# Turning the mask bytes of a graph attention kernel on TensorE as four-byte float32r words instead of two-byte bfloat16 words

## The chip, the cores and the metric

The kernel runs on one NeuronCore of a Trainium2 chip. The metric is the device time of one execution in microseconds (us), lower is better. TensorE is called PE here, its weight loads PEld, VectorE is DVE, ScalarE is ACT, GpSimd is POOL and SyncE is SP.

## The reference

Two graph layers over 8192 nodes with 128 features. The first is an attention with a 0/1 adjacency mask, the second a plain product with the same adjacency.

```python
    h = jnp.maximum(_layernorm(x, axis=-1), 0.0)
    x = x + _L0_gnn_ref(h, adj, L0_gnn_cmt_weight, L0_gnn_W, L0_gnn_a1, L0_gnn_a2)
    h = jnp.maximum(_layernorm(x, axis=-1), 0.0)
    x = x + _L1_gnn_ref(h, adj, L1_gnn_W1, L1_gnn_W2, L1_gnn_b)
```

```python
        Wh = inputs @ W
        f1 = Wh @ a1
        f2 = Wh @ a2
        e = jax.nn.leaky_relu(f1 + f2.T, negative_slope=ALPHA)
        scores = jnp.where(adj > 0, e, NEG_INF)
        att = jax.nn.softmax(scores, axis=-1)
        node_out = jax.nn.relu(att @ Wh)
```

```python
        node = h @ W1
        hw = jnp.einsum('nc,kcf->nkf', h, W2)
        x = jnp.einsum('nk,nkf->nf', node, hw)
        x = adj @ x
        x = x + node @ b
```

## The kernel before

The adjacency is 8192 x 8192 float32 (268 MB), read once. Its 8 x 8 blocks of 1024 x 1024 are walked in 64 half turns: 8 blocks of rows (`ib`), and for each 8 blocks of columns, two (`p` = 0, 1) to a turn `jg`. One half turn works so:

- SP loads the block in two halves of 2 MB into `adj_sb` (four buffers `q`).
- ACT casts it to bytes of 0 or 64 in `m8` (L508, four instructions of 2048 elements a row in a half turn). `m8[:, p, t, n]` has on each of 128 partitions 8 rows `t` of 1024 column bytes.
- PE turns the bytes (`turn_mask`, L751 to L760). It takes two neighbouring bytes as one bfloat16 word and transposes 128 x 128 words at a time; the mode moves the words without arithmetic. A bank of PSUM (`mt_ps0`, `mt_ps1` in turns) takes eight such transposes, and four banks (`k` = 0 to 3, C = 4) make up the half turn. Bank `k` holds the words k, k + 4, k + 8 and so on of all eight rows.
- ACT copies each bank to `mt[:, p, k, :]` (`evict`, L520). When all four are there, they are also stored to `maskT_d` for the second layer (L626, 1 MB).
- DVE forms the attention weights (`weigh`, L1008): per bank two instructions, one per byte of the words (`b_`), each 1024 elements, max(z, q) times the mask byte. It writes one of four buffers of `p_sb`.
- PE multiplies them with the rows of `wh` (L824): per buffer 8 float32 products of 129 columns, each two instructions, added up in `ot_ps`.

A **step** below is one `k` of a half turn: PE turns a bank that is of the step after next, and then does the products of two `p_sb` buffers (32 MATMULs). In the half turns of the last seven blocks of rows, PE, ACT, DVE and POOL also finish one tile of 128 nodes of the block before: layer norm, the sixteen heads of the second layer (L789 on PE, L585 on ACT, sums on POOL), in pieces at k = 0 to 3.

The program of each engine is in a fixed order written out by hand; engines meet by semaphores. `turned` counts banks turned, `evicted` banks copied, `p_ready` buffers weighed, `p_used[r]` buffers multiplied, `adj_cast[q]` casts done, `mt_stored[p]` stores landed.

In the second part (adjacency stage, `gather`, L881) the stored bytes are loaded again, ACT (L612) and DVE (L1048) widen them to float32r words `mask32`, and PE multiplies them, 512 columns at a time, with the messages in `msgs` (float32r too).

Of the kernel before, what the change touches and what calls it, by code (L numbers as in the profile page):

```python
# [38 lines left out]
def build(nc, x, adj, W, a1, a2, W1, W2, b, out):  # L39
# [25 lines left out]
    with ctx:  # L65
# [6 lines left out]
        def sem(name):  # L72
# [6 lines left out]
        msgs_at = nc.sbuf_base - 4 * (NT * (D + 2) + BLK * T // 2 + C * BLK)  # L79
        msgs = nc.alloc_sbuf_tensor_at("msgs", [P, NT, 2, D], FP32R, offset=msgs_at)  # L80
# [10 lines left out]
        ident16 = sb("ident16", [P, P], BF16)  # L91
# [37 lines left out]
            .rearrange("p (s c n b) -> p s c n b", s=2, c=C, b=2)  # L129
# [15 lines left out]
            .rearrange("p (s i c n b) -> p s i c n b", s=4, i=2, c=C, b=2)  # L145
# [217 lines left out]
        def _(pool):  # L363
# [3 lines left out]
            pool.memset(ident16[:, :], 0.0).then_inc(consts, 1)  # L367
            pool.wait_ge(consts, 2)
            for m in (ident, ident16):
                pool.affine_select(out=m[:, :], in_=m[:, :], compare_op=ALU.not_equal, fill=1.0, base=0,  # L370
                                   pattern=[[-1, P]], channel_multiplier=1).then_inc(consts, 1)
# [98 lines left out]
        def _(act):  # L470
# [74 lines left out]
            act.activation(bcol[:, :], fcol[:, :, 1], ACT.Exp, bias=shifts[:, 0:1]).then_inc(setup_act, 1)  # L545
            for h in range(2):
                act.wait_ge(z0_done, h + 1)
                act.activation(zbf[:, h * HB:(h + 1) * HB], hw_ps[h][:, :], ACT.Copy).then_inc(z0_copied, 1)

            evict(1, 1, 0, 0)  # L550
# [6 lines left out]
            act.dma_start(zrow_d, zT[:, :]).then_inc(z_stored, 16)  # L557

# [46 lines left out]
            def convert(ii, first, t):  # L605
                s, r = t // T, t % 2
                for ib in range(2):
                    if not on_dve(first, t, ib):
                        act.wait_ge(masks_in[s % 4], 16 * (ii * (NB // 4) + s // 4 + 1))
                        if not (first and t < 2):  # L610
                            act.wait_ge(conv_used[r][ib], ii * (NT // 2) + t // 2)
                        act.activation(mask32[:, r, ib, :], masks[:, s % 4, ib, t % T // 2, :, t % 2], ACT.Copy)\  # L612
                           .then_inc(conv_act, 1)

            def turn(i, ib, jg, finish, last):
                for p in range(2):
                    n = 2 * i + p
                    for k in range(C):

                        if k < 2:  # L620
                            evict(C * n + k + 2, k + 2, p, 0)
                        elif not (last and p == 1):
                            evict(C * n + k + 2, k - 2, 1 - p, i + p)
# [75 lines left out]
        def _(pe):  # L699
# [49 lines left out]
            def turn_mask(chunk, k, p, casts):  # L749

                if k == 0:  # L751
                    for h in range(2):
                        pe.wait_ge(adj_cast[2 * p + h], casts)
                if not (isinstance(chunk, int) and chunk < 2):
                    pe.wait_ge(evicted, chunk - 1)
                words = mt_ps[k % 2][:, :].bitcast(BF16)
                for t in range(T):
                    ins = pe.transpose(words[:, t * P:(t + 1) * P],  # L758
                                       m8[:, p, t, :].bitcast(BF16)[:, k:BLK // 2:C], ident16[:, :])
                ins.then_inc(turned, 1)  # L760
# [16 lines left out]
            pe.transpose(h_ps[0:NT, D:D + P], zcol[:, :], ident[:, :]).then_inc(setup_pe, 1)  # L777

# [21 lines left out]
            def half_turn(ib, jg, p, finish, last):  # L800
# [6 lines left out]
                for k in range(C):  # L807
                    if k < 2:
                        turn_mask(C * n + k + 2, k + 2, p, 0)
                    elif not (last and p == 1):  # L810
                        turn_mask(C * n + k + 2, k - 2, 1 - p, i + 1 + p)
# [93 lines left out]
        def _(dve):  # L905
# [98 lines left out]
            def weigh(n, i, ib, p, k, b_, tile):  # L1004

                r = 2 * (k % 2) + b_
                dve.wait_ge(p_used[r], 4 * i + 2 * p + k // 2)
                dve.scalar_tensor_tensor(p_sb[:, r, :], zbf[:, bass.ds((ib % 2) * BLK, BLK)],  # L1008
                                         qcol[:, bass.ds(tile + b_, 1)], mtb[:, p, k, :, b_],
                                         ALU.max, ALU.mult).then_inc(p_ready, 1)  # L1010

            def turn(i, ib, jg, finish, last):
                for p in range(2):
                    n = 2 * i + p
                    u = i - IT
                    for k in range(C):
                        c = C * n + k
                        tile = (2 * jg + p) * T + 2 * k
                        dve.wait_ge(evicted, c + 1)
# [11 lines left out]
            def start_weights(ib):  # L1031

                if isinstance(ib, int) and ib == 0:
                    dve.wait_ge(z0_copied, 2)
                else:
                    dve.wait_ge(zb_in, 16 * ib)
                dve.wait_ge(evicted, C * NB * ib + 1)
                for b_ in range(2):
                    weigh(NB * ib, IT * ib, ib, 0, 0, b_, 0)

            def convert(ii, first, t):
                s, r = t // T, t % 2
                for ib in range(2):
                    if on_dve(first, t, ib):
                        dve.wait_ge(masks_in[s % 4], 16 * (ii * (NB // 4) + s // 4 + 1))
                        if not (first and t < 2):
                            dve.wait_ge(conv_used[r][ib], ii * (NT // 2) + t // 2)
                        dve.tensor_copy(mask32[:, r, ib, :], masks[:, s % 4, ib, t % T // 2, :, t % 2])\  # L1048
                           .then_inc(conv_dve, 1)
# [88 lines left out]
```

## Time and profile before

| | us |
|---|---|
| median of 3 runs | 1843.87 (1843.55 to 1845.21) |
| the profiled execution's own time | 1848.05 |
| its span in the trace | 1846.4 |
| PE busy (weight loads PEld) | 1814.0 (1578.9) |
| ACT, DVE, POOL busy | 1328.9, 1202.2, 695.8 |
| start of the attention's products | 60.5 |
| end of the last turned bank | 1310 |

The span is measured from the first to the last instruction of the profiled execution. MATMULs are pipelined, so a MATMUL's recorded duration is longer than its turn on the array: the pace is read from start to start. An instruction of an engine is recorded with its source line; a row names what it writes and reads, the count behind x, and the idle time of the engine just before with what ended it.

### The profile page before, as it was taken

Reading aid. Unit: us, or ns where it says so; the run is one execution under the profiler, and the core shown is the slowest. Engines: PE = TensorE matmul, PEld = TensorE weight load, DVE = VectorE, ACT = ScalarE, POOL = GpSimd, SP = SyncE. Lnnn points to the kernel's source line nnn. Section 1 sums busy time; section 2 is a strip of 40 time slices with the busy share of each in tenths; the row PEclk is TensorE's granted clock in tenths of the full one; section 3 lists DMA queues with packets and bytes.
Section 4 is the critical chain, followed back from the end, with each engine's and each line's share of the span. In section 5 each row is a group of like instructions: output and inputs, shape, how many; then the busy total and the mean of one; then the engine's idle time right before and its main releaser. Section 6 shows DMA issues by size and latency. Waiting matters only on the chain.

```text
span 1846.4 us, 38424 instructions
## 1 busy us (share of the span) xinstructions
PE 1814.0 (98%) x13344; PEld 1578.9 (86%) x13344; DVE 1202.2 (65%) x1519; ACT 1328.9 (72%) x2145; POOL 695.8 (38%) x524
## 2 busy tenths in 40 slices
PE   8999999999999999999999999999999999999998
PEld 5899989889988988998898889889867788888886
DVE  7676677767767776776777677767665543443434
ACT  6766788788788778877887887887456655555554
POOL 0000256556545655664565556446544400000000
PEclk9999999999999999999999999999999999999999
DMA  9788867776776777677767767772933344345330
GB/s 331 293 347 315 325 244 287 288 283 253 292 294 257 272 293 292 241 291 294 271 259 298 288 251 278 291 279 109 384 122 146 146 160 183 139 177 206 148 148 23
DMA packets 105809, 452.19 MB, mean 245 GB/s; under 512 B 6736, under 2 KB 15136, under 8 KB 87968
## 3 DMA queue, kind: packets, MB, share of 16 engines
q1 hardware_dynamic: 86720, 356.53, 51.9%
q10 hardware_dynamic: 12208, 75.62, 10.0%
q0 software_dynamic: 6832, 19.41, 2.9%
q8 instruction: 29, 0.48, 0.1%
q14 instruction: 20, 0.16, 0.0%
HBM read 364.46 MB, written 87.07 MB: 245 GB/s over the span
## 4 chain that ended last, share of the span: by engine, by line
PE 89%; DVE 3%; ACT 2%; issue 2%; SPq 1%; DMA 1%; POOL 1%; DVEq 0%; POOLq 0%; ACTq 0%
PE ot_ps L824 46%; PE mt_ps L881 12%; PE ot_ps L881 12%; PE hw_ps L789 11%; PE mt_ps L758 6%; SPq L292 1%; PE h_ps L784 1%; DVE att L984 1%; DVE p_sb L1008 1%; ACT prod L585 1%; DMA adj_sb<-in_adj_dram 1%; POOL prod L390 1%; DMA keep_d<-keep 1%; ACT wh_mask L508 1%; DVE keep L989 0%
## 5 line engine op out<-in xcount | busy, mean ns | idle before, releaser
L824 PE MATMUL ot_ps<-wh_mask,p_sb 128*128 (+1 forms) x8192 | 978.5, 277 | 9.2 <-DVE p_sb L1008 9.2
L824 PEld LDWEIGHTS ot_ps<-wh_mask,p_sb 128*128 128x128 f32 x8192 | 939.9, 192 | 11.4 <-DVE p_sb L1008 10.9
L1008 DVE SCALAR_TENSOR_TENSOR p_sb<-zb,qcol,mt 128x1024 f32<-128x1024 uint8 (+1 forms) x512 | 771.0, 1536 | 266.0 <-ACT mt L520 218.0
L390 POOL TENSOR_TENSOR prod<-prod 128x1024 f32<-128x1024 f32 (+2 forms) x192 | 404.4, 2106 | 521.0 <-ACT prod L585 503.8
L508 ACT ACTIVATE wh_mask<-adj_sb 128x2048 uint8<-128x2048 f32 x256 | 493.0, 1929 | 1.7 <-ACT mt L520 1.1
L612 ACT ACTIVATE mask<-adj_sb 128x1024 fp32r<-128x1024 uint8 x240 | 255.5, 1065 | 176.5 <-PE ot_ps L881 176.4
L520 ACT ACTIVATE mt<-mt_ps 128x1024 uint16<-128x1024 uint16 x256 | 267.7, 1046 | 136.5 <-PE mt_ps L758 135.8
L1048 DVE CAST mask<-adj_sb 128x1024 fp32r<-128x1024 uint8 x272 | 204.1, 756 | 247.4 <-PE mt_ps L881 245.6
L585 ACT ACTIVATE prod<-hw_ps,node 128x128 f32<-128x128 f32 x1024 | 278.9, 385 | 92.5 <-PE hw_ps L789 91.5
L881 PE MATMUL mt_ps<-mask,msgs 128*128 128x512 f32 x1024 | 283.3, 398 | 3.6 <-DVE mask L1048 2.7
L881 PE MATMUL ot_ps<-mask,msgs 128*128 128x512 f32 x1024 | 275.5, 391 | 0.7
L789 PE MATMUL hw_ps<-wcat,hT 128*128 128x512 f32 x512 | 240.7, 592 | 0.0
L881 PEld LDWEIGHTS mt_ps<-mask,msgs 128*128 128x128 f32 x1024 | 191.7, 188 | 52.7 <-issue 14.3
L881 PEld LDWEIGHTS ot_ps<-mask,msgs 128*128 128x128 f32 x1024 | 192.3, 188 | 43.3 <-issue 3.0
L758 PEld LDWEIGHTS mt_ps<-ident,wh_mask 128*128 128x128 bf16 x2048 | 143.5, 114 | 61.8 <-issue 61.8
L758 PE MATMUL mt_ps<-ident,wh_mask 128*128 128x128 bf16 x2048 | 156.0, 219 | 0.6 <-issue 0.6
L789 PEld LDWEIGHTS hw_ps<-wcat,hT 128*128 128x128 f32 x512 | 88.6, 190 | 61.8 <-issue 61.2
L393 POOL TENSOR_TENSOR msg<-prod 128x128 f32<-128x128 f32 x64 | 82.2, 1284 | 5.0
L418 POOL DMA_DIRECT2D zb<-zrow_d x7 | 3.8, 544 | 179.3 <-DVE p_sb L1008 119.6
L407 POOL TENSOR_TENSOR msg<-msg 128x128 fp32r<-128x128 f32 x56 | 68.0, 1215 | 4.5
L405 POOL CAST msg<-msg 128x128 fp32r<-128x128 f32 x56 | 58.9, 1051 | 9.3 <-POOL msg L393 9.3
L575 ACT ACTIVATE node<-h_ps 128x16 f32<-128x16 f32 x64 | 11.8, 185 | 54.9 <-PE h_ps L784 54.9
(111 smaller groups left out, 610.8 us busy)
## 6 DMA issues: line engine op xcount, KB each, us to landing
adj_sb<-in_adj_dram SPq DMA_DIRECT2D x128, 2048.0 KB, 8.6
maskT_d<-mt ACTq DMA_DIRECT2D x64, 1024.0 KB, 5.2
adj_sb<-maskT_d SPq DMA_DIRECT2D x32, 2048.0 KB, 7.7
keep_d<-keep POOLq DMA_DIRECT2D x64, 128.0 KB, 6.1
p_sb<-keep_d SPq DMA_DIRECT2D x4, 2048.0 KB, 12.2
msg_d<-msg POOLq DMA_DIRECT2D x56, 128.0 KB, 6.0
msgs<-msg_d SPq DMA_DIRECT2D x7, 1024.0 KB, 9.1
wh_mask<-in_x_dram SPq DMA_DIRECT2D x8, 512.0 KB, 9.4
```

The costliest lines, as they stand in the source:

```text
L390: pool.tensor_tensor(prod[:, 0:n, :], prod[:, 0:n, :], prod[:, n:2 * n, :], ALU.add)\
L393: pool.tensor_tensor(msg32[:, :], prod[:, 0, :], prod[:, 1, :], ALU.add).then_inc(prod_read, 1)
L508: ins = act.activation(m8[:, q // 2, t:t + HT // 2, :].rearrange("p t n -> p (t n)"), adj_sb[:, q, part * (HT // 2) * BLK:(part + 1) * (HT ...
L520: act.activation(mt[:, p, k, :], mt_ps[k % 2][:, :].bitcast(U16), ACT.Copy).then_inc(evicted, 1)
L585: ins = act.activation(prod[:, head, :], hw_ps[g % 2][:, j * D:(j + 1) * D], ACT.Copy, scale=node[:, head:head + 1])
L612: act.activation(mask32[:, r, ib, :], masks[:, s % 4, ib, t % T // 2, :, t % 2], ACT.Copy)\
L758: ins = pe.transpose(words[:, t * P:(t + 1) * P], m8[:, p, t, :].bitcast(BF16)[:, k:BLK // 2:C], ident16[:, :])
L789: pe.matmul(hw_ps[g % 2][:, :], hT[:, :], wcat[:, g * HB:(g + 1) * HB], start=True, stop=True)\
L824: ins = pe.matmul(ot_ps[h][:, (t - t0) * ROW:(t - t0 + 1) * ROW], p_sb[:, r, t * P:(t + 1) * P], rows, start=begin and t == t0, stop=end a ...
L881: ins = pe.matmul(acc_ps[2 * ib + h][:, :], msgs[:, ORDER[s] * T + t % T, c, :], mask32[:, r, ib, h * HB:(h + 1) * HB], start=t == 0 and c ...
L1008: dve.scalar_tensor_tensor(p_sb[:, r, :], zbf[:, bass.ds((ib % 2) * BLK, BLK)], qcol[:, bass.ds(tile + b_, 1)], mtb[:, p, k, :, b_], ALU.m ...
L1048: dve.tensor_copy(mask32[:, r, ib, :], masks[:, s % 4, ib, t % T // 2, :, t % 2])\
```

## The change

`turn_mask` reads `m8` through a second name for the same bytes, `m8_words`, typed float32r: four neighbouring bytes are one word. A bank then takes four transposes of 128 x 128 words of four bytes instead of eight of two bytes; it is as full as before (2 KB a partition). Bank `k` now holds every second word (k // 2) of four of the eight rows (k % 2). The identity is a float32r tile, `identr`. Since a weigh needs all eight rows of its byte column, DVE needs two banks, k and k + 1, before an even k; so each bank is turned and evicted one step sooner: at step k the bank of k + 3, not k + 2. A third bank is turned ahead of the loop. The first half of the cast rows (`adj_cast[2 * p]`) is now enough for bank 0, and the second half is waited for at bank 1. DVE and ACT read the bytes of `mt` and of `maskT_d` with a stride of 4 bytes instead of 2.

```diff
+        m8_at = nc.sbuf_base - 4 * (BLK * T // 2 + C * BLK)
+        m8_words = nc.alloc_sbuf_tensor_at("m8_words", [P, 2, T, BLK // 4], FP32R, offset=m8_at)
...
-        ident16 = sb("ident16", [P, P], BF16)
+        identr = sb("identr", [P, P], FP32R)
...
-            .rearrange("p (s c n b) -> p s c n b", s=2, c=C, b=2)
+            .rearrange("p (s c n b) -> p s c n b", s=2, c=2, b=4)
...
+            evict(1, 1, 0, 0)
             for h in range(2):
                 act.wait_ge(z0_done, h + 1)
                 act.activation(zbf[:, h * HB:(h + 1) * HB], hw_ps[h][:, :], ACT.Copy).then_inc(z0_copied, 1)
 
-            evict(1, 1, 0, 0)
...
+            evict(2, 2, 0, 0)
...
-                        act.activation(mask32[:, r, ib, :], masks[:, s % 4, ib, t % T // 2, :, t % 2], ACT.Copy)\
+                        act.activation(mask32[:, r, ib, :], masks[:, s % 4, ib, t % T // 4, :, t % 4], ACT.Copy)\
...
-                        if k < 2:
-                            evict(C * n + k + 2, k + 2, p, 0)
+                        if k == 0:
+                            evict(C * n + 3, 3, p, 0)
                         elif not (last and p == 1):
-                            evict(C * n + k + 2, k - 2, 1 - p, i + p)
+                            evict(C * n + k + 3, k - 1, 1 - p, i + p)
...
-                if k == 0:
-                    for h in range(2):
-                        pe.wait_ge(adj_cast[2 * p + h], casts)
+                if k < 2:
+                    pe.wait_ge(adj_cast[2 * p + k], casts)
                 if not (isinstance(chunk, int) and chunk < 2):
                     pe.wait_ge(evicted, chunk - 1)
-                words = mt_ps[k % 2][:, :].bitcast(BF16)
-                for t in range(T):
+                words = mt_ps[k % 2][:, :].bitcast(FP32R)
+                for t in range(HT):
                     ins = pe.transpose(words[:, t * P:(t + 1) * P],
-                                       m8[:, p, t, :].bitcast(BF16)[:, k:BLK // 2:C], ident16[:, :])
+                                       m8_words[:, p, k % 2 * HT + t, k // 2:BLK // 4:2], identr[:, :])
                 ins.then_inc(turned, 1)
...
+            turn_mask(2, 2, 0, 1)
...
-                    if k < 2:
-                        turn_mask(C * n + k + 2, k + 2, p, 0)
+                    if k == 0:
+                        turn_mask(C * n + 3, 3, p, 0)
                     elif not (last and p == 1):
-                        turn_mask(C * n + k + 2, k - 2, 1 - p, i + 1 + p)
+                        turn_mask(C * n + k + 3, k - 1, 1 - p, i + 1 + p)
...
-                                         qcol[:, bass.ds(tile + b_, 1)], mtb[:, p, k, :, b_],
+                                         qcol[:, bass.ds(tile + b_, 1)], mtb[:, p, k // 2, :, 2 * (k % 2) + b_],
...
-                        dve.wait_ge(evicted, c + 1)
+                        dve.wait_ge(evicted, C * n + 2 * (k // 2) + 2)
```

The order of PE at the start of the attention, before (L758 is the transposes, L824 the products, `h_ps` a small bank of the set-up):

```order
L776 MATMUL h_ps<-wx_sb,small 128x128
L777 MATMUL h_ps<-ident,zcol 64x128
L758 MATMUL mt_ps<-ident,wh_mask 128x128 x8
L824 MATMUL ot_ps<-wh_mask,p_sb 128x129 x16
L758 MATMUL mt_ps<-ident,wh_mask 128x128 x8
```

The same place of the changed program, where L760 is the transposes and L827 the products:

```order
L778 MATMUL h_ps<-wx_sb,small 128x128
L779 MATMUL h_ps<-ident,zcol 64x128
L760 MATMUL mt_ps<-identr,m_words 128x128 x8
L827 MATMUL ot_ps<-wh_mask,p_sb 128x129 x16
L760 MATMUL mt_ps<-identr,m_words 128x128 x4
```

Before, the loop's first bank has eight transposes and the set-up none; now two banks of four stand together here (the extra bank turned ahead, and the loop's first), and every later step has four. An entry of these lists stands for one instruction of the program; a float32 product is two MATMULs in the trace.

The order of ACT in the first rolled turn at k = 1 and k = 2, before, with what each row waits for (L520 evicts a bank, L508 casts, L626 stores, `ISA` and `REGISTER_ALU` set registers):

```order
L520 ACTIVATE mt<-mt_ps 128x1024 [waits turned]
L505 ISA
L508 ACTIVATE wh_mask<-adj_sb 128x2048 [waits turned,adj_in0]
L516 REGISTER_ALU
L518 REGISTER_ALU [waits turned]
L519 REGISTER_ALU [waits p_ready]
L520 ACTIVATE mt<-mt_ps 128x1024 [waits mt_stored1]
L626 ISA [waits evicted]
L626 DMA maskT_d<-mt 128x4096
```

The same place now (L522, L510 and L629 in their stead):

```order
L520 REGISTER_ALU [waits turned]
L521 REGISTER_ALU [waits p_ready]
L522 ACTIVATE mt<-mt_ps 128x1024 [waits mt_stored1]
L507 ISA
L510 ACTIVATE wh_mask<-adj_sb 128x2048 [waits turned,adj_in0]
L518 REGISTER_ALU
L522 ACTIVATE mt<-mt_ps 128x1024 [waits turned]
L629 ISA [waits evicted]
L629 DMA maskT_d<-mt 128x4096
```

The eviction that opens a new `mt` buffer, and so waits for that buffer's store, moved from k = 2 to k = 1; the place of the store itself did not move, and each step still has one eviction.

## Rows read from the trace of the kernel before

**Rows 1.** The page, part 1: busy us, share of the span, instructions.
```profile
PE 1814.0 (98%) x13344; PEld 1578.9 (86%) x13344; DVE 1202.2 (65%) x1519; ACT 1328.9 (72%) x2145; POOL 695.8 (38%) x524
```

**Rows 2.** The page, part 4: shares of the chain that ended last.
```profile
PE 89%; DVE 3%; ACT 2%; issue 2%; SPq 1%; DMA 1%; POOL 1%; DVEq 0%; POOLq 0%; ACTq 0%
PE ot_ps L824 46%; PE mt_ps L881 12%; PE ot_ps L881 12%; PE hw_ps L789 11%; PE mt_ps L758 6%; SPq L292 1%; PE h_ps L784 1%; DVE att L984 1%; DVE p_sb L1008 1%; ACT prod L585 1%; DMA adj_sb<-in_adj_dram 1%; POOL prod L390 1%; DMA keep_d<-keep 1%; ACT wh_mask L508 1%; DVE keep L989 0%
```

**Rows 3.** Busy us by stage, one half turn third: PE, PEld, DVE, ACT, POOL.
```profile
60.00:190.00 130.00, 128.91 (x1261) 128.75 (x1262) 90.65 (x73) 94.73 (x71) 1.10 (x2) 1.00 0.87 333
190.00:1300.00 1110.00, 1102.41 (x9378) 988.65 (x9377) 807.80 (x847) 885.76 (x1544) 609.70 (x435) 1.00 0.72 272
1043.20:1063.30 20.10, 20.10 (x172) 18.02 (x171) 14.70 (x16) 16.14 (x29) 11.71 (x8) 1.00 0.72 274
1300.00:1846.00 546.00, 533.24 (x2399) 427.89 (x2396) 262.64 (x383) 310.72 (x448) 82.48 (x74) 0.99 0.42 162
```

**Rows 4.** The page, part 5, PE: busy us, mean ns | idle before.
```profile
L824 PE MATMUL ot_ps<-wh_mask,p_sb 128*128 (+1 forms) x8192 | 978.5, 277 | 9.2 <-DVE p_sb L1008 9.2
...
L758 PE MATMUL mt_ps<-ident,wh_mask 128*128 128x128 bf16 x2048 | 156.0, 219 | 0.6 <-issue 0.6
```

**Rows 5.** Timeline of PE, one half turn: start us, us, what.
```profile
1043.23 0.61 PE L758 MATMUL mt_ps<-ident,wh_mask 128*128 128x128 bf16 x8
1043.67 3.79 PE L824 MATMUL ot_ps<-wh_mask,p_sb 128*128 x32
1047.30 0.61 PE L758 MATMUL mt_ps<-ident,wh_mask 128*128 128x128 bf16 x8
...
1055.56 0.41 PE L784 MATMUL h_ps<-wcat,hT 128*128 128x144 f32 x2
...
1061.60 1.88 PE L789 MATMUL hw_ps<-wcat,hT 128*128 128x512 f32 x4
1063.32 0.61 PE L758 MATMUL mt_ps<-ident,wh_mask 128*128 128x128 bf16 x8
```

**Rows 6.** Timeline of PE, transposes of the results at 1485 us.
```profile
1485.22 1.03 PE L853 MATMUL hw_ps<-ident,prod 128*128 128x128 f32 x8
1486.09 0.60 PE L853 MATMUL ot_ps<-ident,prod 128*128 128x128 f32 x4
```

**Rows 7.** Timeline of PE, adjacency stage: 512-column products.
```profile
1432.44 1.08 PE L881 MATMUL mt_ps<-mask,msgs 128*128 128x512 f32 x4
1433.36 1.07 PE L881 MATMUL ot_ps<-mask,msgs 128*128 128x512 f32 x4
```

**Rows 8.** Weight loads by form: busy us, mean ns | idle before.
```profile
L824 PEld LDWEIGHTS ot_ps<-wh_mask,p_sb 128*128 128x128 f32 x8192 | 939.9, 192 | 11.4 <-DVE p_sb L1008 10.9 <-issue 0.5
L881 PEld LDWEIGHTS ot_ps<-mask,msgs 128*128 128x128 f32 x1024 | 192.3, 188 | 43.3 <-issue 3.0
...
L853 PEld LDWEIGHTS hw_ps<-ident,prod 128*128 128x128 f32 x32 | 3.7, 140 | 1.6 <-ACT prod L657 1.2
...
L766 PEld LDWEIGHTS h_ps<-ident,ext 128*2 128x2 f32 x1 | 0.1, 81 | 0.5 <-DVE ext L942 0.5
```

**Rows 9.** Timeline of ACT, the same half turn.
```profile
1052.18 1.02 ACT L520 ACTIVATE mt<-mt_ps 128x1024 uint16<-128x1024 uint16 x1 [1.22 <-PE mt_ps L758]
...
1054.90 0.27 ACT L561 ACTIVATE hT<-h_ps 128x128 f32<-128x128 f32 x1
...
1060.68 1.07 ACT L520 ACTIVATE mt<-mt_ps 128x1024 uint16<-128x1024 uint16 x1
```

**Rows 10.** Timeline of DVE, the same half turn.
```profile
1045.89 3.07 DVE L1008 SCALAR_TENSOR_TENSOR p_sb<-zb,qcol,mt 128x1024 f32<-128x1024 uint8 x1 [0.25 <-PE ot_ps L824]
...
1061.90 1.28 DVE L1008 SCALAR_TENSOR_TENSOR p_sb<-zb,qcol,mt 128x1024 f32<-128x1024 uint8 x1 [4.57 <-ACT mt L520]
```

**Rows 11.** The page, part 6: KB each, median us to landing.
```profile
adj_sb<-in_adj_dram SPq DMA_DIRECT2D x128, 2048.0 KB, 8.6
maskT_d<-mt ACTq DMA_DIRECT2D x64, 1024.0 KB, 5.2
```

More of the change, by code:

```diff
@@ L144, in build @@
         masks = adj_sb[:, :, :].rearrange("p s n -> p (s n)").bitcast(U8)\
-            .rearrange("p (s i c n b) -> p s i c n b", s=4, i=2, c=C, b=2)
+            .rearrange("p (s i c n b) -> p s i c n b", s=4, i=2, c=2, b=4)
         masks_w = adj_sb[:, :, :].rearrange("p s n -> p (s n)").bitcast(U16)\
@@ L366, in _ @@
             pool.memset(ident[:, :], 0.0).then_inc(consts, 1)
-            pool.memset(ident16[:, :], 0.0).then_inc(consts, 1)
+            pool.memset(identr[:, :].bitcast(FP32), 0.0).then_inc(consts, 1)
             pool.wait_ge(consts, 2)
-            for m in (ident, ident16):
+            for m in (ident, identr):
                 pool.affine_select(out=m[:, :], in_=m[:, :], compare_op=ALU.not_equal, fill=1.0, base=0,
@@ L1016, in turn @@
                     for k in range(C):
-                        c = C * n + k
                         tile = (2 * jg + p) * T + 2 * k
-                        dve.wait_ge(evicted, c + 1)
+                        dve.wait_ge(evicted, C * n + 2 * (k // 2) + 2)
                         weighed = p == 0 and k == 0 and isinstance(jg, int) and jg == 0
@@ L1036, in start_weights @@
                     dve.wait_ge(zb_in, 16 * ib)
-                dve.wait_ge(evicted, C * NB * ib + 1)
+                dve.wait_ge(evicted, C * NB * ib + 2)
                 for b_ in range(2):
@@ L1047, in convert @@
                             dve.wait_ge(conv_used[r][ib], ii * (NT // 2) + t // 2)
-                        dve.tensor_copy(mask32[:, r, ib, :], masks[:, s % 4, ib, t % T // 2, :, t % 2])\
+                        dve.tensor_copy(mask32[:, r, ib, :], masks[:, s % 4, ib, t % T // 4, :, t % 4])\
                            .then_inc(conv_dve, 1)
```

## The prediction

> **What bounds the kernel now.** I began with the busy times of the page: TensorE (PE) is busy 98% of the span, the next engine, ACT, 72% [rows 1]. Since a busy PE can hide waits of others, I read the chain that ended last: 89% of it is PE, and the mask transposes (L758) alone are 6%, about 0.055 x 1846 = 102 us [rows 2]. Then the table by stage. The attention runs from 60 to 1310 us and all transposes lie in it; PE is busy 1102 of 1110 us in its long part, and in the first block 129 of 130 us [rows 3]. Of idle time before the products PE shows 9.2 us in all, before the transposes 0.6 us [rows 4]. So whatever PE is spared in the attention shortens the kernel, as long as nobody else becomes late.
>
> Next, the pace. Durations overlap, so I took starts. One half turn: the transposes of a bank start at 1043.23 and the products at 1043.67, thus 0.44 us for eight, 0.056 us each (0.448 for eight, also from the group's length, (0.61 - 0.22)/7 = 0.056, with the mean of a transpose from [rows 4]). The 32 products take until 1047.30, 3.63 us or 0.113 each; a step is 4.07 us [rows 5]. The half turn is four such steps plus the finishing of a tile, 20.09 us from 1043.23 to 1063.32.
>
> **The change part by part.**
>
> *The transposes.* 64 half turns x 4 banks = 256 banks. Before, 256 x 8 x 0.056 = 114.7 us of PE. After, 256 x 4 = 1024 transposes of 128 x 128 four-byte words typed float32r. The trace has no such instruction, so I bound it by the nearest rows, in turn:
> - A bfloat16 transpose, 0.056 us [rows 5]. Nothing here moves 128 columns quicker; this is the lower end.
> - A float32 transpose of the same shape (L853): eight start at 1485.22 and the next group at 1486.09, 0.87/8 = 0.109 us [rows 6]. It is the upper end if the type makes no difference.
> - What the type does to a product: four float32 products of 512 columns (L789) take from 1061.60 to 1063.32, 0.43 us each [rows 5]; four float32r products of as many columns (L881) take from 1432.44 to 1433.36, 0.23 us each [rows 7]. Float32r streams its columns about once where float32 takes two turns. The same factor on the transpose gives 0.109 x 0.23/0.43 = 0.058 us.
> - The weight load must keep up, since here the data is the stationary operand. A load of 2 columns takes 81 ns, one of 128 columns in a float32 transpose 140 ns, so the columns of a transpose cost some 59 ns; in products of four-byte type the load is 188 to 192 ns, so 107 to 111 ns [rows 8]. A transpose pays the shorter one, whichever of the two types: at least the float32 transpose does.
>
> I take 0.060 us, the longer of 0.058 and 0.059 rounded up: the stride of 8 bytes between words is not new (the two-byte words had it too). A bank is then 0.240 us instead of 0.448, 0.208 us less, and 256 banks save 53.2 us. At 0.056 they save 57.3 us, at 0.109 3.1 us.
>
> The Trainium skill speaks against this in "TensorE: Matmul & The Clock Gate", sections "LDWEIGHTS (loading the stationary operand)" and "Weight-path perf modes — Fast Weight Load (FWL) and DoubleRow": the fast load is for types other than FP32, and a plain load of P columns is given as P/1.2 ns, some 107 ns for 128. By that, four transposes would be bound by their loads at 0.43 us, and the change would be worth some 5 us, as an estimate from that page. The load of 140 ns in the float32 transposes [rows 8] is less than the 81 + 107 = 188 ns that this rule would make of it, so the trace does not bear it out for transposes, while the loads of products agree with it.
>
> *The banks a step sooner.* Each step still has one bank turned and one evicted. The bank turned at step k waits for the eviction of the bank two before it, as before. DVE before needed the eviction of a step for both its even and its odd bank. For the even bank it still needs the one of the same step (the pair's second bank is evicted where the first was); for the odd one nothing is waited for any more. In the half turn shown ACT evicts at 1060.68, held up by the scaling of heads and a cast, and DVE sat idle 4.57 us for that before L1008 at 1061.90 [rows 9, 10]. This is the odd bank's eviction; it now holds up nobody at that point. PE did not wait for it, so the gain is cover, priced at 0.
>
> The eviction that opens an `mt` buffer waits for the store of that buffer, issued at k = 2 of the half turn before. It comes one step sooner, at k = 1. From issue there are three steps of 4 us plus 3.4 us of finishing, over 12 us; the store lands in 5.2 us [rows 5, 11]. Priced at 0; were the cover gone, each us late would hold the banks behind that eviction, then DVE, then PE. The other queues keep their order: SP's loads wait for casts, whose waits for turned banks are met sooner. The store of 1 MB and the loads of 4 MB go out once a half turn as before. In the first block, where they moved 333 GB/s at 0.87 of the DMA engines [rows 3], a half turn falls from 16.3 us (four steps of 4.07) to 15.5 us and asks for 333 x 16.3/15.5 = 350 GB/s; a load lands in 8.6 us [rows 11] and a buffer is loaded once in two half turns, so I price this at 0.
>
> *The strides.* DVE reads mask bytes at a stride of 4 instead of 2 in 512 weighs, ACT and DVE in 512 conversions of the second part. Each byte was fetched apart before too; I expect 1.28 us for a weigh left alone as now [rows 10]. If it grew, the cover is large: DVE is busy 14.7 of 20.1 us of a half turn [rows 3], and eight weighs share the rest.
>
> *The set-up* has one bank more turned ahead (0.24 us, and taken from the end), an eviction moved into a wait of ACT, and an identity of four bytes. Within 0.5 us: 0.
>
> **Does the saving stay?** A half turn of PE falls from 20.09 to 20.09 - 0.83 = 19.26 us. In it ACT is busy 16.14, DVE 14.70, POOL 11.71 [rows 3]; all fit. The tightest meeting is at k = 2: ACT's relu at 1054.90 ends at 1055.17, and PE needs it at 1055.56, 0.39 us later [rows 5, 9]. Both follow the turned bank of that step, so both come 0.2 us sooner. The longest weigh, 3.07 us beside POOL's sums [rows 10], does not shrink; where PE waits for a weigh today (9.2 us in nine places) it may wait some tenths longer, 1 to 2 us in all.
>
> Sum against the profiled execution: span 1846.4 - 53.2 + 1 = 1794 us, own time 1848.05 - 52 = 1796. The median of the runs is 4.2 us under the profiled time: 1843.87 - 53.2 + 1 = 1791.7, say 1791.5 us. The likeliest case's own range is 1785 (0.056 us a transpose) to 1800.
>
> **The rivals.** Measurement tells about 0.2%, 3.7 us, from no change.
> 1. *The word is four bytes, and PE pays for it* (0.19). The loads run at the 107 ns of other four-byte loads, or the transposes at the 109 ns of float32 ones. For: every four-byte stream here but float32r products costs double. Against: the ratio in rows 5 and 7 and the 140 ns load. Price: 1024 x 0.109 = 111.6 against 114.7 us, 3 us saved: 1841 us. With the word of the page named above on loads it is this case that one would expect. Signs: 0.05 faster, 0.12 within 0.2%, 0.02 slower.
> 2. *PE's saving turns into waits for ACT or DVE* (0.12). ACT is busy 16.1 us of a half turn and waits the rest for PE in fixed order; if half of its waits do not shrink, or weighs grow by the stride, 0.4 us a half turn come back: 64 x 0.4 = 26 us, so 1791 + 26 = 1817 us. For: DVE's weighs stretch beside POOL. Against: the room of 3 us above.
> 3. *Slower: a float32r transpose of 128 columns costs as much as the smallest float32r product seen* (0.09). That product is 512 columns at 0.23 us; if short ones cost no less, a bank is 0.92 us, 256 x (0.92 - 0.448) = 121 us more: 1965 us. It decides as soon as one transpose costs more than 2 x 0.056 = 0.112 us; each further ns is 1.02 us. Against: the load and column prices add up in every other shape shown, and float32 transposes of this shape need only 0.109.
> 4. The forecast: 0.60.
>
> **How the numbers follow.** Faster by over 0.2%: 0.60 + 0.12 + 0.05 = 0.77. Within: 0.12. Slower: 0.02 + 0.09 = 0.11. The forecast and rival 2 hold 0.72, so the range must reach to rival 1: from 1784 (0.056 a transpose and some of the nine waits gone) to 1842.
>
> **What would show it.** The transposes, now 1024, from start to start: 0.06 us says the main step is right, 0.109 rival 1, over 0.112 rival 3. Their weight load: about 140 ns, against 190 for rival 1. The half turn of 20.09 should be 19.26 us; the first block should be over some 7 us sooner. PE's idle time before L824 should stay near 9 us; 35 us there is rival 2. DVE's waits for the eviction, such as the 4.57 us above, should fall, and the evictions themselves stay at 1.02 to 1.07 us. The second part should last the same. I am wrong if the price of a four-byte word is one that rows 6 to 8 don't show.

## The result and the profile after

The changed kernel takes 1853.08 us (median; 1852.17 to 1857.36), the kernel before, measured beside it, 1844.54 us. The ratio is 1.0050, with a 95% interval of 1.0038 to 1.0062: slower by half a per cent, 8.5 us, where 1791.5 us was forecast. The profiled execution has a span of 1852.4 us (before 1846.4).

First the lines of the page that answer to [rows 1] and [rows 4], busy us, mean ns and idle time before (the lines moved: L760 is the transposes, L827 the products, L1011 the weighs, L522 the evictions):

```profile
PE 1823.7 (98%) x12320; PEld 1598.2 (86%) x12320; DVE 1155.7 (62%) x1519; ACT 1328.9 (72%) x2145; POOL 631.3 (34%) x524
...
L827 PE MATMUL ot_ps<-wh_mask,p_sb 128*128 (+1 forms) x8192 | 981.3, 277 | 7.1 <-DVE p_sb L1011 7.1
...
L1011 DVE SCALAR_TENSOR_TENSOR p_sb<-zb,qcol,mt 128x1024 f32<-128x1024 uint8 (+1 forms) x512 | 725.2, 1442 | 275.0 <-PE ot_ps L827 266.2
L392 POOL TENSOR_TENSOR prod<-prod 128x1024 f32<-128x1024 f32 (+2 forms) x192 | 332.1, 1730 | 589.9 <-ACT prod L588 579.4
...
L522 ACT ACTIVATE mt<-mt_ps 128x1024 uint16<-128x1024 uint16 x256 | 267.5, 1045 | 135.6 <-PE mt_ps L760 134.9
...
L760 PE MATMUL mt_ps<-identr,m_words 128*128 128x128 f32 x1024 | 219.9, 338 | 0.3 <-ACT mt L522 0.2
L760 PEld LDWEIGHTS mt_ps<-identr,m_words 128*128 128x128 f32 x1024 | 164.8, 196 | 52.4 <-issue 52.2
```

There are 1024 transposes instead of 2048, but PE is busy 10 us more, not less. The recorded mean of a transpose is 338 ns (it was 219), of its weight load 196 ns. The waits of PE for a weigh fell from 9.2 to 7.1 us: the order did what it should, and the loss is in PE's own work (recorded means overlap, so they say that, but not what an instruction costs). The timeline of PE over one half turn, as in [rows 5]:

```profile
1050.57 1.03 PE L760 MATMUL mt_ps<-identr,m_words 128*128 128x128 f32 x4
1051.43 3.81 PE L827 MATMUL ot_ps<-wh_mask,p_sb 128*128 x32
1055.00 0.73 PE L760 MATMUL mt_ps<-identr,m_words 128*128 128x128 f32 x4
1055.57 3.80 PE L827 MATMUL ot_ps<-wh_mask,p_sb 128*128 x32
1059.12 0.73 PE L760 MATMUL mt_ps<-identr,m_words 128*128 128x128 f32 x4
...
1070.83 1.03 PE L760 MATMUL mt_ps<-identr,m_words 128*128 128x128 f32 x4
```

The four transposes of a bank start at 1055.00 and the products at 1055.57: 0.57 us, 0.14 us for each transpose, where eight took 0.44. Some of it is given back, since the group starts beside the last product before it: from the first of 32 products to the next group there are now 3.57 us (1051.43 to 1055.00) instead of 3.63. A step is 4.12 us (1055.00 to 1059.12) instead of 4.07, and a half turn 20.26 us (1050.57 to 1070.83) instead of 20.09. 0.17 us in 64 half turns is some 11 us.

The stages, as in [rows 3] (us; busy PE, PEld, DVE, ACT, POOL; clock; share of the DMA engines; GB/s):

```profile
60.00:193.00 133.00, 132.37 (x1150) 132.02 (x1150) 90.82 (x73) 95.47 (x73) 1.10 (x2) 1.00 0.87 329
193.00:1309.00 1116.00, 1109.52 (x8485) 1005.41 (x8484) 759.71 (x847) 884.32 (x1540) 544.87 (x435) 1.00 0.71 270
1309.00:1852.00 543.00, 532.12 (x2385) 426.36 (x2383) 263.90 (x384) 310.45 (x449) 82.78 (x74) 1.00 0.43 164
```

PE is busy 99% of both parts of the attention, as before, and no other engine is busier than before. TensorE's granted clock is 1.00 (its level of 2.4 GHz) throughout. So it is neither the clock nor a new wait. From the list of waits (us in total, times, longest), what DVE waits for now, and PE for DVE:

```profile
DVE p_sb L1011 <- PE ot_ps L827: 266.2, 180, 3.1
...
PE ot_ps L827 <- DVE p_sb L1011: 7.1, 7, 1.1
...
DVE p_sb L1011 <- ACT mt L522: 5.6, 3, 3.1
```

The same wait for an eviction in the kernel before:

```profile
DVE p_sb L1008 <- ACT mt L520: 218.0, 53, 4.7
```

DVE waits for an eviction 5.6 us instead of 218.0, and now it waits for PE to free a buffer. That is the engine one wants it to wait for. A weigh lasts 1442 ns in the mean instead of 1536, and POOL's sums 1730 instead of 2106. The likely reason is that the two meet less, since DVE weighs at other moments; no run was made to show it.

### The profile page after: what moved, and what is told of

It is laid out like the page before. It is cut to its first block, busy times and chain, and to the rows that moved or that the text cites. A ratio compares the mean times of both kernels' runs of the same rounds, so it can differ in the third digit from the quotient of the medians.

```text
span 1852.4 us, 36207 instructions
## 1 busy us (share of the span) xinstructions
PE 1823.7 (98%) x12320; PEld 1598.2 (86%) x12320; DVE 1155.7 (62%) x1519; ACT 1328.9 (72%) x2145; POOL 631.3 (34%) x524
## 4 chain that ended last, share of the span: by engine, by line
PE 90%; DVE 3%; ACT 2%; issue 2%; SPq 1%; DMA 1%; POOL 0%; DVEq 0%; ACTq 0%; POOLq 0%
PE ot_ps L827 47%; PE ot_ps L884 12%; PE mt_ps L884 12%; PE hw_ps L792 11%; PE mt_ps L760 6%; SPq L294 1%; PE h_ps L787 1%; DVE att L987 1%; ACT wh_mask L510 1%; DMA adj_sb<-in_adj_dram 1%; ACT prod L588 1%; DVE p_sb L1011 0%; DVE keep L992 0%; PE h_ps L799 0%; ACT ut L605 0%
## 5 line engine op out<-in xcount | busy, mean ns | idle before, releaser
L827 PE MATMUL ot_ps<-wh_mask,p_sb 128*128 (+1 forms) x8192 | 981.3, 277 | 7.1 <-DVE p_sb L1011 7.1
L827 PEld LDWEIGHTS ot_ps<-wh_mask,p_sb 128*128 128x128 f32 x8192 | 938.7, 192 | 8.9 <-DVE p_sb L1011 8.4
L1011 DVE SCALAR_TENSOR_TENSOR p_sb<-zb,qcol,mt 128x1024 f32<-128x1024 uint8 (+1 forms) x512 | 725.2, 1442 | 275.0 <-PE ot_ps L827 266.2
L392 POOL TENSOR_TENSOR prod<-prod 128x1024 f32<-128x1024 f32 (+2 forms) x192 | 332.1, 1730 | 589.9 <-ACT prod L588 579.4
L510 ACT ACTIVATE wh_mask<-adj_sb 128x2048 uint8<-128x2048 f32 x256 | 492.9, 1929 | 2.0 <-ACT mt L522 1.0
L615 ACT ACTIVATE mask<-adj_sb 128x1024 fp32r<-128x1024 uint8 x240 | 255.6, 1066 | 173.6 <-PE ot_ps L884 173.5
L522 ACT ACTIVATE mt<-mt_ps 128x1024 uint16<-128x1024 uint16 x256 | 267.5, 1045 | 135.6 <-PE mt_ps L760 134.9
L792 PE MATMUL hw_ps<-wcat,hT 128*128 128x512 f32 x512 | 240.7, 592 | 0.0
L760 PE MATMUL mt_ps<-identr,m_words 128*128 128x128 f32 x1024 | 219.9, 338 | 0.3 <-ACT mt L522 0.2
L760 PEld LDWEIGHTS mt_ps<-identr,m_words 128*128 128x128 f32 x1024 | 164.8, 196 | 52.4 <-issue 52.2
L792 PEld LDWEIGHTS hw_ps<-wcat,hT 128*128 128x128 f32 x512 | 88.6, 190 | 61.8 <-issue 61.2
L395 POOL TENSOR_TENSOR msg<-prod 128x128 f32<-128x128 f32 x64 | 90.2, 1409 | 5.0
```

What stands on the lines that cost most here:

```text
L392: pool.tensor_tensor(prod[:, 0:n, :], prod[:, 0:n, :], prod[:, n:2 * n, :], ALU.add)\
L395: pool.tensor_tensor(msg32[:, :], prod[:, 0, :], prod[:, 1, :], ALU.add).then_inc(prod_read, 1)
L510: ins = act.activation(m8[:, q // 2, t:t + HT // 2, :].rearrange("p t n -> p (t n)"), adj_sb[:, q, part * (HT // 2) * BLK:(part + 1) * (HT ...
L522: act.activation(mt[:, p, k, :], mt_ps[k % 2][:, :].bitcast(U16), ACT.Copy).then_inc(evicted, 1)
L760: ins = pe.transpose(words[:, t * P:(t + 1) * P], m8_words[:, p, k % 2 * HT + t, k // 2:BLK // 4:2], identr[:, :])
L792: pe.matmul(hw_ps[g % 2][:, :], hT[:, :], wcat[:, g * HB:(g + 1) * HB], start=True, stop=True)\
```

## The experiments

Two theories after the result. **Stride**: a four-byte weight load whose words do not lie side by side is slow, whatever the type. **Type**: a float32r transpose of 128 columns costs 0.14 us by itself. And a third question: what the new order costs or gives alone.

**Neighbouring words.** Each transpose reads 128 neighbouring words:

```diff
-                                       m8_words[:, p, k % 2 * HT + t, k // 2:BLK // 4:2], identr[:, :])
+                                       m8_words[:, p, k % 2 * HT + t, k // 2 * P:k // 2 * P + P], identr[:, :])
```

> The changed kernel, with each float32r transpose reading 128 neighbouring four-byte words instead of every second one (so other bytes are turned than the reference needs; the work is the same). In the changed kernel transposes follow each other at 0.140 us. If the stride of 8 bytes is what slows them, the pace falls to 0.109 us or less, perhaps 0.06, and the kernel to 1840 us (at 0.109) or 1795 us (at 0.06). If the type float32r in a transpose is what costs, the pace stays 0.140 and the time 1853 us.

Measured: 1811.18 us, ratio 0.9826 (0.9810 to 0.9841). Its weight loads, by form:

```profile
L760 PEld LDWEIGHTS mt_ps<-identr,m_words 128*128 128x128 f32 x1024 | 111.5, 141 | 58.7 <-issue 58.3 <-ACT wh_mask L510 0.5
```

141 ns instead of 196. That is the load of the float32 transposes in [rows 8]. The stride alone costs 42 us here, so type alone cannot be the cause. But 1811 us lies between the two times that I had worked out: single starts in the trace stand 0.084 us apart once a group runs, not 0.06. That is 0.056 us less than the 0.14 of the changed kernel, and the load is 0.055 us shorter: the pace fell by what the load lost.

**Every fourth word.**

```diff
-                                       m8_words[:, p, k % 2 * HT + t, k // 2:BLK // 4:2], identr[:, :])
+                                       m8_words[:, p, :, :].rearrange("p t n -> p (t n)")
+                                       [:, (k % 2 * HT + min(t, 2)) * (BLK // 4) + k // 2:
+                                           (k % 2 * HT + min(t, 2) + 2) * (BLK // 4):4], identr[:, :])
```

> The changed kernel with float32r transposes that read every fourth word (16 bytes apart) instead of every second (other bytes than needed). If the stride costs, the pace rises from 0.140 to 0.17 us or more; if only the type counts, it stays 0.140.

Measured: 1854.85 us, a single run. The loads, by form:

```profile
L760 PEld LDWEIGHTS mt_ps<-identr,m_words 128*128 128x128 f32 x1024 | 166.1, 198 | 52.4 <-issue 52.2 <-ACT wh_mask L510 0.2
```

198 ns against 196, the step unchanged. The expectation of the stride theory was wrong in its form: the price is not in proportion to the gap. Every second word and every fourth load equally slowly; what counts up to there is whether they are neighbours.

**The same words as float32.**

```diff
-        m8_words = nc.alloc_sbuf_tensor_at("m8_words", [P, 2, T, BLK // 4], FP32R, offset=m8_at)
+        m8_words = nc.alloc_sbuf_tensor_at("m8_words", [P, 2, T, BLK // 4], FP32, offset=m8_at)
...
-                words = mt_ps[k % 2][:, :].bitcast(FP32R)
+                words = mt_ps[k % 2][:, :]
...
-                                       m8_words[:, p, k % 2 * HT + t, k // 2:BLK // 4:2], identr[:, :])
+                                       m8_words[:, p, k % 2 * HT + t, k // 2:BLK // 4:2], ident[:, :])
```

> The changed kernel with the same words, same stride and same order, but typed float32 with the float32 identity. If the type float32r is what costs, the pace becomes the 0.109 us of the other float32 transposes and the time 1844 us or a little less (four times 0.031 us less in each of 256 banks, but for the part of the first one that is covered: some 9 us below 1853). If the stride costs, the load is slowed here too and the pace stays near 0.140, the time near 1853 us.

Measured: 1836.51 us, ratio 0.9951 (0.9937 to 0.9965). The loads by form, then the timeline of PE at one bank:

```profile
L760 PEld LDWEIGHTS mt_ps<-ident,m_words 128*128 128x128 f32 x1024 | 150.5, 203 | 52.7 <-issue 52.4 <-ACT wh_mask L510 0.3
```

```profile
1045.45 0.64 PE L760 MATMUL mt_ps<-ident,m_words 128*128 128x128 f32 x4
1045.93 1.95 PE L827 MATMUL ot_ps<-wh_mask,p_sb 128*128 x16
```

The load is as slow as with float32r (203 ns), so the stride is paid by both types. Four transposes take 0.48 us, 0.12 each, hardly more than the 0.109 of [rows 6]. Taking off the 81 ns that even a load of two columns takes [rows 8], the load is 203 - 81 = 122 ns, so the pace of float32 is that of its load. With float32r it is longer than its load: 0.14 us against 196 - 81 = 115 ns. Both theories held a part: the stride makes the load long, and the type decides how much is paid on top. The plainer type is the quicker one here, by 16.6 us.

**Float32 with neighbouring words** (on the kernel with a permuted cast that follows below):

> The same with float32 instead of float32r transposes, words neighbouring. The load falls from 0.203 to 0.141 us, but the pace is then set by the two passes of float32, 0.109 us. Four times 0.109 instead of some 0.118: 256 x 0.03 = 8 us under the 1836.5 us of float32 with the stride, so 1829 us; if type counted for nothing beside the stride it would be 1811 us.

Measured: 1828.02 us, ratio 0.9908 (0.9893 to 0.9923), as worked out. The loads by form, then the timeline of PE:

```profile
L760 PEld LDWEIGHTS mt_ps<-ident,m_words 128*128 128x128 f32 x1024 | 124.4, 142 | 58.7 <-issue 58.3 <-ACT wh_mask L511 0.4
```

```profile
1045.23 0.60 PE L760 MATMUL mt_ps<-ident,m_words 128*128 128x128 f32 x4
1045.67 3.74 PE L827 MATMUL ot_ps<-wh_mask,p_sb 128*128 x32
```

Four transposes take 0.44 us, 0.11 each, though the load less the 81 ns is only 61 ns. So in float32 both runs fit a pace that is the longer of load and passes (122 and 0.12, then 0.109), and in float32r both are some 25 ns above the load (115 and 0.14, 60 and 0.084).

This completes the square, in us: float32r 1853.1 with stride and 1811.2 without, float32 1836.5 and 1828.0. Without the stride float32r wins by 17 (0.084 against 0.109 us a transpose); with it, it loses by 17 (0.14 against 0.12).

**The order alone.** The order of the changed kernel, with eight bfloat16 transposes in each bank. The bytes then lie in another order, so DVE and ACT read each column of bytes in two runs of 512; those lines, and the bfloat16 identity, are left out here:

```diff
...
-                words = mt_ps[k % 2][:, :].bitcast(FP32R)
-                for t in range(HT):
-                    ins = pe.transpose(words[:, t * P:(t + 1) * P],
-                                       m8_words[:, p, k % 2 * HT + t, k // 2:BLK // 4:2], identr[:, :])
+                words = mt_ps[k % 2][:, :].bitcast(BF16)
+                for w in range(2):
+                    for t in range(HT):
+                        ins = pe.transpose(words[:, (w * HT + t) * P:(w * HT + t + 1) * P],
+                                           m8[:, p, k % 2 * HT + t, :].bitcast(BF16)[:, k // 2 * 2 + w:BLK // 2:C],
+                                           ident16[:, :])
```

> The changed kernel's order (each bank a step sooner, pairs of banks waited for, half of the cast rows for each bank), with the eight bfloat16 transposes of before in each bank; the bytes lie in another order within a bank, and DVE and ACT read them in two runs. If the order costs nothing and the loss is all in the transposes, the time is that of before, 1844.5 us, or up to 2 us less for the waits taken away. If the order costs something, it is above 1846 us.

Measured: 1841.61 us, ratio 0.9986 (0.9977 to 0.9995). The transposes by form, and from the list of waits:

```profile
L762 PE MATMUL mt_ps<-ident,wh_mask 128*128 128x128 bf16 x2048 | 156.7, 220 | 0.3 <-ACT wh_mask L511 0.2
```

```profile
DVE p_sb L1014 <- PE ot_ps L830: 239.9, 148, 3.0
...
PE ot_ps L830 <- DVE p_sb L1014: 7.1, 6, 1.3
```

The order is worth 2.9 us of its own (with the reading in two runs, whose price was not taken apart), and PE's waits for a weigh are 2.1 us shorter (9.2 before, 7.1 now). So the transposes lose 11.5 us, which agrees with the 11 us read from the half turns, and 11.5 - 2.9 = 8.6 is the result (8.5 measured).

**Neighbours by a permuted cast.** ACT's cast writes the even words of all rows first, then the odd ones, so that each transpose finds its words side by side (the shapes of the names `m8` and `m8_words` change with it, left out here):

```diff
...
-                ins = act.activation(m8[:, q // 2, t:t + HT // 2, :].rearrange("p t n -> p (t n)"),
-                                     adj_sb[:, q, part * (HT // 2) * BLK:(part + 1) * (HT // 2) * BLK], ACT.Copy,
-                                     scale=EDGE)
+                rows = adj_sb[:, q, part * (HT // 2) * BLK:(part + 1) * (HT // 2) * BLK]
+                ins = act.activation(m8[:, q // 2, :, t:t + HT // 2, :].rearrange("p c t (m b) -> p c (t m) b", b=4),
+                                     rows.rearrange("p (m c b) -> p c m b", c=2, b=4), ACT.Copy, scale=EDGE)
...
+                                       m8_words[:, p, k // 2, k % 2 * HT + t, :], identr[:, :])
```

> The changed kernel with the cast of ACT writing the bytes so that the words of a transpose are neighbours (its destination runs over the even words of all rows, then over the odd ones; its source is read in pieces of four floats), and float32r transposes of neighbouring words; the output is the reference's. If the stride of the weight load is the whole cause, the transposes run at 0.084 us as in the run with neighbouring words, and the time is 1811 us, 1.8% under the kernel before. If the cast becomes slower for its broken access (1.93 us now, four in a half turn; ACT has some 3 us of room in a half turn of 19.3), the gain shrinks once a cast takes over 2.6 us.

Measured: 1810.62 us, ratio 0.9818 (0.9804 to 0.9831): 34 us under the kernel before, the quickest of the kernels here, with the reference's output. Groups of instructions, and the timeline of PE:

```profile
L827 PE MATMUL ot_ps<-wh_mask,p_sb 128*128 (+1 forms) x8192 | 982.2, 278 | 11.2 <-DVE p_sb L1011 11.2
...
L511 ACT ACTIVATE wh_mask<-adj_sb 128x2048 uint8<-128x2048 f32 x256 | 493.3, 1931 | 1.4 <-ACT mt L522 1.0 <-DMA adj_sb<-in_adj_dram 0.3
...
L760 PEld LDWEIGHTS mt_ps<-identr,m_words 128*128 128x128 f32 x1024 | 111.5, 141 | 58.7 <-issue 58.2 <-ACT wh_mask L511 0.5
```

```profile
999.94 3.81 PE L827 MATMUL ot_ps<-wh_mask,p_sb 128*128 x32
1003.50 0.53 PE L760 MATMUL mt_ps<-identr,m_words 128*128 128x128 f32 x4
1003.87 2.02 PE L827 MATMUL ot_ps<-wh_mask,p_sb 128*128 x16
```

The cast did not notice (1931 ns, before 1929). Four transposes take 0.37 us, a step 3.93 us (999.94 to 1003.87) instead of 4.07; 256 x 0.14 = 36 us. PE's waits for a weigh rose to 11.2 us, the 1 to 2 us more that had been foreseen.

**Transposes spread between the products.** The long load might hide beside the products, if each transpose stood alone before every second product of a buffer (the lines that hand the transposes over are left out):

```diff
...
+                                if turn and b_ == 0 and t % 2 == 0:
+                                    turn(t // 2)
                                 ins = pe.matmul(ot_ps[h][:, (t - t0) * ROW:(t - t0 + 1) * ROW],
...
```

> The changed kernel (stride of two words) with the four transposes of a bank not in one group but one each before every second product of the first p_sb buffer. If what limits is the sum of the weight loads on one side and of the passes on the other, the long loads hide beside the products and a step falls from 4.13 to about 4.0 us: 1820 us. If each switch between the types costs by itself (the changed kernel shows 0.18 instead of 0.11 us for the first product behind a group), four switches instead of one cost more: 1850 us or above.

Measured: 1905.95 us, ratio 1.0331 (1.0315 to 1.0347). The timeline of PE:

```profile
1050.09 0.32 PE L761 MATMUL mt_ps<-identr,m_words 128*128 128x128 f32 x1
1050.24 0.68 PE L837 MATMUL ot_ps<-wh_mask,p_sb 128*128 128x129 f32 x4
1050.68 0.31 PE L761 MATMUL mt_ps<-identr,m_words 128*128 128x128 f32 x1
1050.83 0.68 PE L837 MATMUL ot_ps<-wh_mask,p_sb 128*128 128x129 f32 x4
```

One transpose and two products (four MATMULs) take 0.59 us (1050.09 to 1050.68). Single starts of products stand 0.112 us apart, so four are 0.45, and a transpose alone costs 0.14 us. In the group it costs (4.12 - 32 x 0.112)/4 = 0.13. Nothing is hidden by the spreading.

The same with neighbouring words:

> Neighbouring words as in e6_perm and the transposes spread as in e9_inter. If loads and passes are two sums that hide each other: 32 products of 0.112 us and four passes of 0.056 make a step of 3.81 us, 17 us under e6_perm, so 1794 us. If each switch costs by itself, some 0.05 us more for each transpose, so 30 us and more above e6_perm: 1840 us or above.

Measured: 1883.48 us, ratio 1.0212 (1.0196 to 1.0228). The timeline of PE, then a line of the list of waits:

```profile
1052.29 0.30 PE L761 MATMUL mt_ps<-identr,m_words 128*128 128x128 f32 x1
1052.43 0.66 PE L837 MATMUL ot_ps<-wh_mask,p_sb 128*128 x4
1052.85 0.31 PE L761 MATMUL mt_ps<-identr,m_words 128*128 128x128 f32 x1
1052.99 0.66 PE L837 MATMUL ot_ps<-wh_mask,p_sb 128*128 x4
1053.40 0.30 PE L761 MATMUL mt_ps<-identr,m_words 128*128 128x128 f32 x1
```

```profile
PE h_ps L794 <- ACT hT L564: 38.7, 54, 1.0
```

With neighbouring words a transpose and its four MATMULs take 0.555 us ((1053.40 - 1052.29)/2), so a transpose alone costs 0.555 - 0.448 = 0.107 us, 0.43 for four, where the step of the grouped kernel spends 3.93 - 32 x 0.112 = 0.35. So the idea of two sums that hide each other is refuted, and here four changes between the types cost 0.08 us a bank more than one. But both spread kernels lost more than that (53 and 73 us), and the list of waits names why: PE waited 38.7 us for ACT's relu of a tile. The last transpose of a bank ends some 1.4 us later when they are spread (3 x 0.555 + 0.30 us after the first starts, instead of 0.53). At k = 2 ACT then evicts later, and the cast and relu queued behind on ACT come later too; the 0.39 us of room in [rows 5, 9] is gone. The last run of this kind takes the spreading away at k = 2 only (the line is shown against the run before):

```diff
-                        turn = turn_mask(C * n + k + 3, k - 1, 1 - p, i + 1 + p, True)
+                        turn = turn_mask(C * n + k + 3, k - 1, 1 - p, i + 1 + p, k != 2)
```

> The kernel with neighbouring words and spread transposes, but at step k = 2 the four stand in one group again, so that ACT's eviction, cast and relu of that step are not later. In the run with all steps spread PE waited 39 us for the relu. If that wait was a consequence of the bank being turned late at k = 2, it goes, and what is left over 1810.6 us is the price of switching types: three quarters of 256 x 0.075 us = 14 us, so 1825 us. If switching costs nothing and the wait was all, the time is 1811 us or less; if the wait has another cause, 1870 us or more.

Measured: 1829.98 us, ratio 0.9919 (0.9903 to 0.9936). The timeline of PE at a relu:

```profile
1043.26 0.48 PE L794 MATMUL h_ps<-wcat,hT 128*128 128x144 f32 x2
1043.58 1.88 PE L799 MATMUL hw_ps<-wcat,hT 128*128 128x512 f32 x4
```

The wait is gone from the list, and the time fell by 53.5 us, of which only 64 x 0.08 = 5 us are the spreading that was taken away: the late relu cost more than its 38.7 us of idle time. What stays is 19 us over the grouped kernel, 0.10 us for each of 192 spread banks, where 0.075 was expected. The starts give 0.08, 15 us. The rest lies where PE takes up the relu's result: L794 holds 0.32 us there (1043.26 to 1043.58), in the grouped kernel 0.25 (its L787 at 1046.69, L792 at 1046.94), and 56 such places at 0.07 us are 4 us.

**A stride in the products.** On the kernel with the permuted cast:

```diff
-                                                p_sb[:, r, t * P:(t + 1) * P], rows, start=begin and t == t0, stop=end and t == t1 - 1)
+                                                p_sb[:, r, t:BLK:T], rows, start=begin and t == t0, stop=end and t == t1 - 1)
```

> The kernel with neighbouring words, whose float32 products in the attention load every eighth column of p_sb as weights instead of 128 neighbours (the output is of other columns; the work is the same). If a stride slows every four-byte weight load by the 0.057 us seen in the transposes, a product's load goes from 0.192 to 0.25 us, its streaming from 0.11 to 0.17, and PE becomes bound by it: 8192 x 0.055 = 450 us more, 2260 us. If the slow load belongs to transposes only, the loads stay at 0.19 us and the time at 1811 us.

Measured: 2839.44 us, a single run. The loads by form, then the timeline of PE:

```profile
L827 PEld LDWEIGHTS ot_ps<-wh_mask,p_sb 128*128 128x128 f32 x8192 | 1979.5, 335 | 1.5 <-DVE p_sb L1011 1.2 <-issue 0.2
```

```profile
999.76 4.69 PE L827 MATMUL ot_ps<-wh_mask,p_sb 128*128 x19
1004.21 0.53 PE L760 MATMUL mt_ps<-identr,m_words 128*128 128x128 f32 x4
```

The load of a product goes from 192 to 335 ns and its pace from 0.112 to 0.24 us: 1029 us more for 8192 MATMULs are 0.126 each, and the rows show 19 starts in 4.45 us, the last gap a short one before the transposes. The slow load is no matter of transposes, and the addition of 0.057 us was the wrong form: taking the 81 ns of a tiny load off, 111 ns become 254, somewhat over double, as 60 become 115 to 122 in the transposes.

## Why the prediction was wrong

- **What bounds the kernel** was right. PE's own time decided each version: where four transposes took 0.14 us less of a step, the kernel won 34 us; where a half turn grew by 0.17 us, it lost 11 on the transposes (8.5 with what the order gave).
- **The price of a transpose** was the step that failed: "I take 0.060 us ... the stride of 8 bytes between words is not new (the two-byte words had it too)". It was 0.14 us. Three things were in it. First, the stride is not new, but the two-byte load suffers little from it and the four-byte load does: 196 against 141 ns, which is 42 us of the kernel. Loads of two-byte words took 114 ns for every fourth word (L758, below) and 104 ns for neighbours (L705, products of zeros in the set-up), and the transposes kept to 0.056 us with it. My row for the load, the 140 ns of L853, reads neighbouring words; it was the nearest by type and shape, but not by access. Second, I let the pace be the longer of load and pass. That fits the float32 transposes, but with neighbouring float32r words it gives 0.060, and 0.084 us was found. Third, part of the group lies beside the product before it, which I had not counted and which gives some 0.06 us a bank back. With these terms the sum comes near: 256 x (4 x 0.14 - 0.448 - 0.06) = 13 us more, less 2.9 for the order, 10 us against 8.5 measured.

The two-byte loads, from the list by form of the kernel before:

```profile
L758 PEld LDWEIGHTS mt_ps<-ident,wh_mask 128*128 128x128 bf16 x2048 | 143.5, 114 | 61.8 <-issue 61.8
...
L705 PEld LDWEIGHTS hw_ps<-zeros 128*128 128x128 bf16 x80 | 8.1, 104 | 11.9 <-issue 2.8 <-POOL eps L374 2.6 <-ACT wcat L528 0.6
```

- **The rivals.** The third had the sign and the point of decision (over 0.112 us a transpose) right and its price too high by far (0.23, so 1965 us); it had 0.09. Its mechanism, a least cost of short float32r products, was not the one at work. The first rival's mechanism, a load that binds, was the true one, but its row (107 ns) again had no stride in it. Its other price, float32 transposes at 0.109 us and 1841 us, was measured too: 1828 us. The order gave 2.9 us of the 13 us between them, and the rest fits a term that neither sum had: 32 products behind a group of float32 transposes last 3.74 us, behind one of bfloat16 3.79 [rows 5], by which I estimate 256 x 0.05 = 13 us. The range, up to 1842 us, had its upper end at the price of float32 transposes, a row with neighbouring words; it did not cover a load with an access that no row showed. The prediction named this itself as what would make it wrong: a price that rows 6 to 8 don't show.
- **The sums** come out but for two small ones: 57.3 us saved gives 1787 us, not 1785, and 6% of the span is 111 us, nearer to the 114.7 of the pace than the 102 that was written. Nothing hangs on them.
- **The page on loads.** The Trainium skill gives some 107 ns for a plain load of 128 columns ("TensorE: Matmul & The Clock Gate", section "LDWEIGHTS (loading the stationary operand)"). For transposes of neighbouring four-byte words the runs show about 60 ns above a tiny load, so it is too dear; with a stride they show 115 to 122 ns, and products of neighbouring words 111 ns, near it. That section makes no difference by stride; the runs show one.
- **The banks a step sooner**, priced at 0, gave 2.9 us; DVE's wait for the odd bank went as foreseen. **The other engines** had the room that was claimed: with neighbouring words, at 1811 us, PE's waits for weighs grew by 2 us only. **The strides of DVE and ACT** cost nothing: evictions last 1045 ns, conversions 1066 and 757 ns on the page, as before.
- **The relu at k = 2** was named as the tightest meeting. It held in the changed kernel, since bank and relu moved together, and it broke where an experiment moved only the bank: 38.7 us of waits.

**Open:** why float32r transposes follow each other some 25 ns later than their load less the 81 ns of a tiny one (84 against 60 ns, 0.14 us against 115 ns), where float32 ones follow at 0.12 us against 122 ns; and why a load of words that are not neighbours is slow. No run tells whether it is the type of the data or of the identity. The permuted cast whose source is whole and whose destination is in pieces was not run.

## What to carry to other kernels

Before PE is given wider words, ask how the words of the stationary operand lie: a four-byte weight load of words that are not neighbours took about twice as long (115 against 60 ns above a tiny load in transposes, 254 against 111 in products), and it can be cheap to let an engine with room write them side by side (here ACT's cast, at no cost). Price an operation by a row of the same type, shape and access; if the access has no row, put the upper bound at least at the double of the load, as these runs show. Keep transposes of another type than the products in one group (spreading them cost 0.08 us a bank with neighbouring words, and hid nothing with a stride), and watch what waits on their last one: a bank turned 1.4 us later in each tile cost some 48 us, more than the work that was moved.

## What was not expected of the hardware

- A four-byte load of 128 columns in a float32r transpose: 141 ns for neighbouring words, 196 ns for every second, 198 ns for every fourth. In a float32 product: 192 ns for neighbours, 335 ns for every eighth.
- Float32r transposes follow at 0.084 us (neighbours) and 0.14 us (stride), float32 ones at 0.109 and 0.12 us: the order of the types turns round with the access.
- A float32r transpose between float32 products costs 0.11 us alone, against some 0.09 us in a group of four.
- After a group of transposes of another type the products start late: 32 of them last 3.79 us behind bfloat16, 3.81 behind float32r and 3.74 behind float32.
